# Causal rounds with two key projections one step further apart, and a norm's constant added by GpSimd

## The chip, the cores and the metric

The kernel runs on one core of a Trainium2 chip. The core has four engines that compute, each with its own instruction queue: TensorE (PE, with PEld for its weight loads), VectorE (DVE), ScalarE (ACT) and GpSimd (POOL). SyncE (SP) issues most DMAs. They meet at semaphores only. The metric is the device time of one execution in microseconds (us), as the median of several runs.

## The reference, cut to what matters

A transformer block over x of shape 4 x 1024 x 128 (four batches, 1024 tokens, 128 features), in this order:

```
mod = (silu(c) @ wmod)                       # six 128-vectors per batch: sa, ca, ga, sb, cb, gb
h = layernorm(x) * (1 + ca) + sa             # "norm 1"
x = x + ga * attention_1(h)                  # one head of width 128, no mask, all 1024 keys
h = layernorm(x) * (1 + cb) + sb             # "norm 2", first part (eps 1e-5)
y = rmsnorm(h) * g1                          # "norm 2", second part (eps 1e-6)
h = h + attention_2(y) @ wo                  # causal, 16 query heads, 4 key heads of width 64, rotary
h = h + moe(rmsnorm(h) * g2)                 # 8 experts, one of two picked per token
x = x + gb * h
```

layernorm is (x - mean) / sqrt(var + eps) over the 128 features, and rmsnorm is x / sqrt(mean(x*x) + eps). The rotary part multiplies q by a cosine table and a half-swapped q by a sine table, and adds the two; the same for k.

## The kernel before

The kernel goes through four stages: a start (modulation, norm 1 of batch 0), attention 1 over 32 query tiles (to about 237 us), 16 causal rounds (238 to 1108 us), and the routing with the experts (to the end). The change touches the rounds and the norms.

**Rounds.** One round is one batch and one key head with its four query heads. It has 36 steps, nine for a query head. In each step PE computes four 128x128 blocks of scores (`scoresB`, L1199 to L1203), ACT takes the exponential (L917) and copies it to 16 bit (L905), POOL subtracts the copy to get the low half (L707), and five steps later PE multiplies both halves with the values (`values_parts`, L1221 to L1223, two halves of a step each).

**Side work.** Beside this a round prepares the next one, and finishes the one before, in *entries* that are spread over its steps by tables: "max" (scores again, for the row maxima; PE L1125 and L1128, DVE L1608 or L1610), "k", "q", "r", "v" (projections for the next round: keys, queries, the rotated part, values; PE L1113 or L1107), "turn" and "out" (output projection of the round before), "row" (the maxima transposed; read by ACT, L897). The table `PROJ` gives the step of each projection:

```
PROJ = {0: ("k", 0), 1: ("k", 1), 3: ("q", 0, 0), 5: ("r", 0, 0), 7: ("q", 0, 1), 9: ("r", 0, 1), 11: ("v",),
HIGH_AT = {4: 0, 12: 1, 22: 2}
LOW_AT = {5: 0, 15: 1, 25: 2}
```

PE fills a PSUM bank for each entry and DVE reads it in the same order. There are three side banks. Entry number i of a round uses bank i modulo 3, and PE may fill it only when entry i - 3 has been read. So the order of entries sets who waits for whom:

| | steps 0 to 9, entries in order (E: maxima of the head after next, pieces 0 to 5; L: of the next head, pieces 6 to 9) |
|---|---|
| before | L6 k0, L7 k1, L8, L9 q00, E0, E1 r00 row, E2, E3 q01, E4 E5, L6 r01 |
| after | L6 k0, L7, L8 k1, L9, E0 q00, E1 row, E2 r00, E3, E4 E5 q01, L6 r01 |

Commas part the steps; k0 and k1 are the two halves of the keys. Reading a k entry takes three DVE instructions (L1583, L1585, L1587), q one (L1597), r two (L1600, L1602), a max one. In a step with one entry PE does the scores, both halves of the values, then the entry. With two or more it does the scores, the first entry, the first half of the values, the second entry, the second half, and what is left.

`HIGH_AT` and `LOW_AT` say at which step ACT (`high_half`, L876) and POOL (`low_half`, L680) split the finished keys (number 0) and queries (1, 2) into high and low halves; then SP copies them into place by DMA (`spread_k`, `spread_q`). Between these SP sends each head's row of maxima (`spread_row`, L481), which the next head's first scores wait for.

**Norms.** Each norm is a chain over engines: DVE centres (L1373, L1376), ACT squares (L759, L776), DVE sums the squares of each token, scales the sum by 1/128 and adds eps (`variance`, L1383 and L1386), POOL raises it to the power -0.5 (`power`, L595), DVE multiplies (L1406, L1426). There are twelve such chains: norm 1 of four batches, and both parts of norm 2 of four batches. Seven run in the start and in attention 1, five in the rounds. `NORM_V`, `NORM_A` and `NORM_P` say at which round and step DVE, ACT and POOL take their part: DVE's `variance` stands at step 4 of rounds 0 and 1, step 24 of round 3, step 28 of round 6 and step 14 of round 8; other DVE parts at step 4 of rounds 2, 6 and 7.

Of the kernel before, what the change touches and what calls it, by code (L numbers as in the profile page):

```python
# [12 lines left out]
ALU = mybir.AluOpType  # L13
ACT = mybir.ActivationFunctionType
AX = mybir.AxisListType

P = 128
B, S, D = 4, 1024, 128
# [15 lines left out]
WE = 2 * HID + 2 * D  # L34
DW = D + 1
LN_EPS, RMS_EPS = 1e-5, 1e-6
A_SCALE = float(1.0 / np.sqrt(8.0).astype(np.float32))
NKV = B * HKV
HALVES = 2
# [32 lines left out]
def reader(entry):  # L72
# [1 line left out]
    return READER[entry[0]]  # L74


PROJ = {0: ("k", 0), 1: ("k", 1), 3: ("q", 0, 0), 5: ("r", 0, 0), 7: ("q", 0, 1), 9: ("r", 0, 1), 11: ("v",),
        13: ("q", 1, 0), 15: ("r", 1, 0), 17: ("q", 1, 1), 19: ("r", 1, 1)}
OUTP = {21: ("turn", 0), 23: ("turn", 1), 25: ("turn", 2), 27: ("turn", 3), 30: ("out", 0), 33: ("out", 1)}

HIGH_AT = {4: 0, 12: 1, 22: 2}
LOW_AT = {5: 0, 15: 1, 25: 2}


INPUT_AT = {0: {29: (1, 0)}, 1: {31: (1, 1)}, 4: {29: (2, 0)}, 5: {31: (2, 1)}, 8: {33: (3, 0)}, 9: {29: (3, 1)}}
# [92 lines left out]
def build(nc, x, cT, wmod, w_qkvT, w_projT, b_proj, g1, g2, w_kv, w_o, router_w, router_b, w_exp, consts,  # L178
          cos_t, sin_t, out):
    ctx = ExitStack()  # L180
    with ctx:
# [3 lines left out]
        def sem(name):  # L185
            return ctx.enter_context(nc.semaphore(name))
# [65 lines left out]
        n1 = tiles(carve(S))  # L252
# [14 lines left out]
        sq1 = tiles(arena[:, 14 * S:15 * S])  # L267
# [5 lines left out]
        sqh = tiles(arena[:, 16 * S:17 * S])  # L273
        sq2 = [tiles(arena[:, 24 * S:25 * S]), tiles(arena[:, 12 * S:13 * S])]
# [46 lines left out]
        st1, st2 = sb("st1", [P, 4, NT]), [sb("st2a", [P, 4, NT]), sb("st2b", [P, 4, NT])]  # L321
        rstd1, rstd2 = sb("rstd1", [P, NT]), [sb("rstd2a", [P, NT]), sb("rstd2b", [P, NT])]
# [5 lines left out]
        epsb = sb("epsb", [P, 2, NT])  # L328
# [34 lines left out]
        n1_V, n1_P, n1_A = sem("norm1_vec"), sem("norm1_pool"), sem("norm1_act")  # L363
        n2_v, n2_n, n2_P, n2_s = [sem("norm2_vec0"), sem("norm2_vec1")], sem("norm2_n"), sem("norm2_gated"), sem("norm2_scaled")
        xsum, n2_pow = sem("x1_with_rows"), [sem("norm2_power0"), sem("norm2_power1")]
        n2_sq, n2_out = [sem("norm2_squares0"), sem("norm2_squares1")], sem("norm2_done")
# [35 lines left out]
        fin, out_done, zero_in, fill_ready = sem("fin"), sem("out_done"), sem("zero_in"), sem("fill_ready")  # L402

        N1V = 4
        own_sum, eps_set = sem("sum_of_squares"), sem("eps_set")
        NCONST, NLATE = 2, 7
        block = ctx.enter_context(nc.Block())

# [179 lines left out]
        def _(pool):  # L588
# [2 lines left out]
            pool.memset(ones16[:, :], 1.0)  # L591
            pool.memset(every[:, :], 1.0).then_inc(e_z, 1)

            def power(dst, st):
                return pool.tensor_tensor(dst[:, :], st[:, 3, :], mhalf, ALU.pow)  # L595

            def norm1_power(c):

                pool.wait_ge(n1_V, N1V * c + 3)
                power(rstd1, st1).then_inc(n1_P, 1)  # L600

            def gated(c):

# [12 lines left out]
            def norm2_power(c, part):  # L616

                pool.wait_ge(n2_v[part], (3 * c + 3, c + 1)[part])
                power(rstd2[part], st2[part]).then_inc(n2_pow[part], 1)

            def scaled(c):

# [96 lines left out]
            for k in range(2):  # L719
# [4 lines left out]
                src = hres[:, 2 * k + 1, :, :]  # L724
# [13 lines left out]
            for t in range(ETILES):  # L738
                k = t % YSLOTS
# [12 lines left out]
        def _(act):  # L752
# [3 lines left out]
            def norm1_squares(c):  # L756

                act.wait_ge(n1_V, N1V * c + 2)
                act.activation(sq1, n1, ACT.Square).then_inc(n1_A, 1)  # L759

            def norm2_squares(c, part):

                if part == 0:
                    act.wait_ge(n2_v[0], 3 * c + 2)
                    if c == 3:
                        act.wait_ge(n2_v[1], 3)
                    src = n2 if c < 2 else hres[:, c, :, :]
                else:
                    act.wait_ge(n2_s, 2 * c + 2)
                    if c > 0:  # L770
                        act.wait_ge(n2_v[1], c)
                    if c >= 2:
                        act.wait_ge(n2_v[0], 3 * c + 3)
                    src = hres[:, c, :, :]
                dst = sqh if (c, part) in ((2, 0), (2, 1), (3, 0), (3, 1)) else sq2[part]
                act.activation(dst, src, ACT.Square).then_inc(n2_sq[part], 1)  # L776

            def norm2_out(c):

# [52 lines left out]
            for t in range(NL):  # L832
                b, i = divmod(t, NT)
                r = t % 3
# [3 lines left out]
                if t >= 3:  # L838
                    act.wait_ge(a_pl, t - 2)
                act.activation(pf0[:, r, :], psS[:, t % 2, :], ACT.Exp, scale=A_SCALE).then_inc(a_E, 1)  # L840
                if 3 <= i < 7 and b + 1 < B:
# [514 lines left out]
        def _(v):  # L1356
# [21 lines left out]
                if cut.stop == NT:  # L1378
                    ins.then_inc(n, 1)

            def variance(n, sq, st, eps):

                v.tensor_reduce(st[:, 2, :], sq, AX.X, ALU.add).then_inc(own_sum, 1)  # L1383
                own_sums[0] += 1
                v.wait_ge(own_sum, own_sums[0])
                v.scalar_tensor_tensor(st[:, 3, :], st[:, 2, :], 1.0 / D, epsb[:, eps, :], ALU.mult, ALU.add).then_inc(n, 1)  # L1386

            own_sums = [0]

            def norm1_a(c):  # L1390

# [6 lines left out]
            def norm1_b(c):  # L1398

                v.wait_ge(n1_A, c + 1)  # L1400
                variance(n1_V, sq1, st1, 0)

            def norm1_c(c):

# [12 lines left out]
            def norm2_b(c):  # L1417

                v.wait_ge(n2_sq[0], c + 1)
                variance(n2_v[0], sq2[0] if c < 2 else sqh, st2[0], 0)  # L1420

            def norm2_c(c, cut=slice(0, NT)):

# [6 lines left out]
            def norm2_d(c):  # L1430

                v.wait_ge(n2_sq[1], c + 1)
                variance(n2_v[1], sq2[1] if c < 2 else sqh, st2[1], 1)

            def part_low(c, k):

# [86 lines left out]
            for t in range(NL):  # L1523
# [18 lines left out]
                if t in (5, 6):  # L1542
                    k = (2, 5)[t - 5]
# [171 lines left out]
            for b in range(B):  # L1715
                src = hres[:, b, :, :]
# [92 lines left out]
            for b in range(B):  # L1809
                r = hres[:, b, :, :]  # L1810
# [22 lines left out]
            for t in range(ETILES):  # L1833
                k = t % 4
# [92 lines left out]
```

## Time and profile before

| | |
|---|---|
| median of 3 runs | 1326.16 us (1324.26 to 1326.85) |
| profiled execution | 1324.32 us, its span 1322.5 us |
| busy share of the span | PE 84%, DVE 80%, POOL 76%, ACT 66% |
| busy us | PE 1116.2, DVE 1053.8, POOL 998.5, ACT 872.8 |

The span goes from the first to the last instruction. A busy share is a mean over four stages that have different limits, so it does not say what a change in one stage is worth. A row of the trace gives the start of an instruction, its duration, its engine, line and operands; in square brackets stands how long the engine was idle before it and whose work ended the idle time.

### The profile page before, as it was taken

Reading aid. Unit: us, or ns where it says so; the run is one execution under the profiler, and the core shown is the slowest. Engines: PE = TensorE matmul, PEld = TensorE weight load, DVE = VectorE, ACT = ScalarE, POOL = GpSimd, SP = SyncE. Lnnn points to the kernel's source line nnn. Section 1 sums busy time; section 2 is a strip of 40 time slices with the busy share of each in tenths; the row PEclk is TensorE's granted clock in tenths of the full one; section 3 lists DMA queues with packets and bytes.
Section 4 is the critical chain, followed back from the end, with each engine's and each line's share of the span. In section 5 each row is a group of like instructions: output and inputs, shape, how many; then the busy total and the mean of one; then the engine's idle time right before and its main releaser. Section 6 shows DMA issues by size and latency. Waiting matters only on the chain.

```text
span 1322.5 us, 36076 instructions
## 1 busy us (share of the span) xinstructions
PE 1116.2 (84%) x14984; PEld 839.5 (63%) x14984; DVE 1053.8 (80%) x2180; ACT 872.8 (66%) x1508; POOL 998.5 (76%) x783
## 2 busy tenths in 40 slices
PE   4979895899999899999999999999999997600891
PEld 2768682566776667767677776776767776600881
DVE  6588765889888898989989889898898875592675
ACT  3656671698888688878888888887888894100330
POOL 3555874698898788989899898798888996226454
PEclk8889998899999899999999999999999999555996
DMA  6240013121222211213112131121211200022793
GB/s 219 50 140 2 2 44 86 42 77 43 71 55 56 61 38 52 58 60 77 38 52 54 49 87 43 53 61 42 77 38 26 62 3 2 0 88 74 219 303 145
DMA packets 49247, 90.85 MB, mean 69 GB/s; under 512 B 8896, under 2 KB 19136, under 8 KB 48832
## 3 DMA queue, kind: packets, MB, share of 16 engines
q1 hardware_dynamic: 46128, 81.21, 21.5%
q0 software_dynamic: 2960, 7.38, 2.1%
q8 instruction: 117, 1.92, 0.6%
q14 instruction: 42, 0.34, 0.1%
HBM read 43.96 MB, written 13.01 MB: 43 GB/s over the span
## 4 chain that ended last, share of the span: by engine, by line
PE 61%; DVE 20%; POOL 7%; issue 4%; SPq 3%; ACT 2%; DMA 2%; POOLq 0%; DVEq 0%; ACTq 0%
PE psT L1125 6%; PE psS L1200 5%; PE psS L1199 5%; PE psT L1113 5%; PE psS L1221 5%; PE psS L1222 5%; PE psS L1223 4%; PE psT L1148 3%; PE psO L1125 3%; PE psO L1200 3%; PE psO L1199 3%; DVE pmax L1608 2%; POOL rows_in L735 2%; DVE psT L1585 2%; DVE arena L1587 2%
## 5 line engine op out<-in xcount | busy, mean ns | idle before, releaser
L707 POOL TENSOR_TENSOR probs<-arena,probs 128x512 f16<-128x512 f32 x576 | 656.7, 1161 | 109.2 <-ACT probs L905 104.9
L905 ACT ACTIVATE probs<-arena 128x512 f16<-128x512 f32 x576 | 362.0, 628 | 14.1
L1221 PE MATMUL psS<-vb,probs 128*128 128x65 f16 x2304 | 302.9, 193 | 3.5 <-POOL probs L707 1.2
L1222 PE MATMUL psS<-vb,probs 128*128 128x64 f16 x2304 | 304.1, 194 | 0.0
L1223 PE MATMUL psS<-vb,probs 128*128 128x65 f16 x2304 | 302.2, 192 | 0.0
L917 ACT ACTIVATE arena<-psS 128x512 f32<-128x512 f32 x384 | 226.1, 589 | 105.9 <-PE psS L1203 59.1
L1221 PEld LDWEIGHTS psS<-vb,probs 128*128 128x128 f16 x2304 | 220.4, 97 | 71.6 <-issue 11.2
L1222 PEld LDWEIGHTS psS<-vb,probs 128*128 128x128 f16 x2304 | 215.7, 97 | 47.7 <-issue 0.5
L1608 DVE TENSOR_REDUCE pmax<-psT 128x1 f32<-128x512 f32 (+1 forms) x311 | 198.1, 641 | 28.9 <-PE psT L1128 14.1
L1223 PEld LDWEIGHTS psS<-vb,probs 128*128 128x128 f16 x2304 | 217.0, 99 | 0.0
L1125 PE MATMUL psT<-arena 128*128 128x512 f16 (+3 forms) x507 | 153.4, 323 | 8.6 <-DVE pmax L1608 4.9
L1200 PE MATMUL psS<-arena 65*128 65x512 f16 (+1 forms) x448 | 158.2, 353 | 0.0
L1199 PE MATMUL psS<-arena 128*128 128x512 f16 (+1 forms) x448 | 156.9, 350 | 0.0
L1608 DVE TENSOR_REDUCE pmax<-psO 128x1 f32<-128x512 f32 (+1 forms) x201 | 134.2, 667 | 23.9 <-PE psO L1125 16.2
L917 ACT ACTIVATE arena<-psO 128x512 f32<-128x512 f32 x192 | 112.5, 586 | 25.2 <-PE psO L1200 16.4
L1113 PE MATMUL psT<-arena,wkv 128*128 128x512 f16 x381 | 105.1, 386 | 20.8 <-DVE arena L1587 19.5
L647 POOL TENSOR_TENSOR probs<-arena,probs 128x1024 f16<-128x1024 f32 x32 | 69.4, 2172 | 55.8 <-ACT probs L847 55.7
L1199 PE MATMUL psO<-arena 128*128 128x384 f16 (+2 forms) x320 | 93.7, 293 | 0.0
L958 ACT ACTIVATE arena<-arena 128x256 f32<-128x256 f32 x40 | 16.7, 418 | 112.8 <-DVE arena L1841 112.7
L1125 PE MATMUL psO<-arena 128*128 128x512 f16 (+2 forms) x261 | 85.7, 341 | 5.4 <-DMA arena<-arena 4.6
L1200 PE MATMUL psO<-arena 65*128 65x384 f16 (+2 forms) x320 | 88.4, 295 | 0.0
L1128 PE MATMUL psT<-maskh,identh 128*128 128x128 bf16 x391 | 79.2, 220 | 0.0
(278 smaller groups left out, 2873.2 us busy)
## 6 DMA issues: line engine op xcount, KB each, us to landing
arena<-arena SPq DMA_DIRECT2D x240, 128.0 KB, 2.4
arena<-w_exp_dram SPq DMA_DIRECT2D x40, 384.0 KB, 4.1
arena<-xnT_d SPq DMA_DIRECT2D x16, 512.0 KB, 3.6
wkv<-w_d SPq DMA_DIRECT2D x16, 352.0 KB, 4.1
rows_in<-arena POOLq DMA_DIRECT2D x1, 2580.0 KB, 20.5
arena<-rows_in SPq DMA_DIRECT2D x40, 64.5 KB, 3.3
arena<-x_dram SPq DMA_DIRECT2D x4, 512.0 KB, 5.2
hres<-x_dram SPq DMA_DIRECT2D x4, 512.0 KB, 5.3
```

The costliest lines, as they stand in the source:

```text
L707: pool.tensor_tensor(pl[:, r, :], pf[:, r, :], ph[:, r, :], ALU.subtract).then_inc(lo_P, 1)
L905: act.activation(ph[:, s % RING, :], pf[:, s % RING, :], ACT.Copy).then_inc(b_hi, 1)
L917: act.activation(pf[:, s % RING, :], score_banks[s % SCORES], ACT.Exp).then_inc(b_exp, 1)
L1113: mm = pe.matmul(dst, wkv[:, p, c, w0:w0 + P], xs[:, p, a, h * 512:(h + 1) * 512], start=(k == 0), stop=(k == 2))
L1125: mm = pe.matmul(dst[:, k * w:(k + 1) * w], qA[:, p, g, i * P:(i + 1) * P], kC[:, p, h * 512:h * 512 + w], start=True, stop=not diag)
L1128: mm = pe.matmul(dst[:, (k + 1) * w - P:(k + 1) * w], identh[:, :], maskh[:, :], start=False, stop=True)
L1199: pe.matmul(dst, kA[:, p, j * P:(j + 1) * P], qA[:, p, g, i0 * P:(i0 + n) * P], start=True, stop=False)
L1200: mm = pe.matmul(dst, kB[0:HD + 1, p, j * P:(j + 1) * P], qB[0:HD + 1, p, g, i0 * P:(i0 + n) * P], start=False, stop=not diag)
L1221: pe.matmul(dst, high, vb[:, p, j, 0:OW], start=first, stop=False, skip_group_check=True)
L1222: pe.matmul(dst[:, 0:HD], high, vb[:, p, j, HD + 2:VW], start=False, stop=False, skip_group_check=True)
L1223: mm = pe.matmul(dst, low, vb[:, p, j, 0:OW], start=False, stop=last, skip_group_check=True)
L1608: ins = v.tensor_reduce(pmax[:, e[1] % 2, at[0]:at[0] + 1], src[:, 0:w], AX.X, ALU.max)
```

## The change

It makes two edits that have nothing to do with each other.

The first moves side work. The second half of the keys (k1) goes from step 1 to 2, the first query entry from 3 to 4, its rotated part from 5 to 6, the third from 7 to 8; the split of the keys into halves goes one step later on ACT and POOL. This holds in rounds 0 to 14; round 15 has no projections.

The second moves work in the norms. ACT squares x times 1/sqrt(128), so the sum of the squares is the mean already. DVE keeps only the sum. The addition of eps, 128x8 elements, goes to POOL, which waits for its own addition before it takes the power. DVE's wait for its own sum goes.

```diff
+ROOT = float(1.0 / np.sqrt(float(D)))
...
-PROJ = {0: ("k", 0), 1: ("k", 1), 3: ("q", 0, 0), 5: ("r", 0, 0), 7: ("q", 0, 1), 9: ("r", 0, 1), 11: ("v",),
+PROJ = {0: ("k", 0), 2: ("k", 1), 4: ("q", 0, 0), 6: ("r", 0, 0), 8: ("q", 0, 1), 9: ("r", 0, 1), 11: ("v",),
...
-HIGH_AT = {4: 0, 12: 1, 22: 2}
-LOW_AT = {5: 0, 15: 1, 25: 2}
+HIGH_AT = {5: 0, 12: 1, 22: 2}
+LOW_AT = {6: 0, 15: 1, 25: 2}
...
-            def power(dst, st):
+            powers = [0]
+
+            def power(dst, st, eps):
+                pool.tensor_tensor(st[:, 3, :], st[:, 2, :], epsb[:, eps, :], ALU.add).then_inc(eps_in, 1)
+                powers[0] += 1
+                pool.wait_ge(eps_in, powers[0])
                 return pool.tensor_tensor(dst[:, :], st[:, 3, :], mhalf, ALU.pow)
...
-                act.activation(sq1, n1, ACT.Square).then_inc(n1_A, 1)
+                act.activation(sq1, n1, ACT.Square, scale=ROOT).then_inc(n1_A, 1)
...
-                act.activation(dst, src, ACT.Square).then_inc(n2_sq[part], 1)
+                act.activation(dst, src, ACT.Square, scale=ROOT).then_inc(n2_sq[part], 1)
...
-            def variance(n, sq, st, eps):
-
-                v.tensor_reduce(st[:, 2, :], sq, AX.X, ALU.add).then_inc(own_sum, 1)
-                own_sums[0] += 1
-                v.wait_ge(own_sum, own_sums[0])
-                v.scalar_tensor_tensor(st[:, 3, :], st[:, 2, :], 1.0 / D, epsb[:, eps, :], ALU.mult, ALU.add).then_inc(n, 1)
+            def variance(n, sq, st):
+
+                v.tensor_reduce(st[:, 2, :], sq, AX.X, ALU.add).then_inc(n, 1)
```

## Rows read from the trace of the kernel before

**Rows 1.** The page's chain that ended last: shares of the span by engine.

```profile
PE 61%; DVE 20%; POOL 7%; issue 4%; SPq 3%; ACT 2%; DMA 2%; POOLq 0%; DVEq 0%; ACTq 0%
```

**Rows 2.** Windows: length, busy us (instructions) by engine, granted clock, DMA share, GB/s.

```profile
445.30:449.30 4.00, 3.98 (x30) 2.93 (x31) 3.42 (x6) 1.23 (x2) 0.61 (x1) 0.50 0.20 45
...
852.60:907.20 54.60, 53.10 (x762) 38.30 (x762) 47.80 (x92) 45.03 (x79) 47.20 (x40) 1.00 0.21 55
```

**Rows 3.** Waits in 250 to 1190 us: who waited, total us, times, longest.

```profile
PE psT L1113 <- DVE arena L1587: 15.5, 14, 1.1
...
PE psT L1125 <- DVE pmax L1608: 4.7, 1, 4.7
```

**Rows 4.** Timeline of PE: the fill of q00 in rounds 3, 4, 11 and 12.

```profile
406.65 0.39 PE L1113 MATMUL psT<-arena,wkv 128*128 128x512 f16 x1 [1.11 <-DVE arena L1587]
...
468.49 0.39 PE L1113 MATMUL psT<-arena,wkv 128*128 128x512 f16 x1 [1.11 <-DVE arena L1587]
...
852.67 0.39 PE L1113 MATMUL psT<-arena,wkv 128*128 128x512 f16 x1 [1.10 <-DVE arena L1587]
...
907.29 0.39 PE L1113 MATMUL psT<-arena,wkv 128*128 128x512 f16 x1 [1.11 <-DVE arena L1587]
```

**Rows 5.** Timeline of PE and DVE in round 11, steps 1 to 4.

```profile
848.71 0.81 PE L1113 MATMUL psT<-arena,wkv 128*128 128x512 f16 x3
...
849.28 0.68 DVE L1587 TENSOR_TENSOR arena<-psT,arena 64x512 f32<-64x512 f32 x1
849.35 0.19 PE L1221 MATMUL psS<-vb,probs 128*128 128x65 f16 x1
...
849.54 0.38 PE L1199 MATMUL psO<-arena 128*128 128x512 f16 x1
...
849.89 0.67 DVE L1608 TENSOR_REDUCE pmax<-psO 128x1 f32<-128x512 f32 x1
...
850.49 0.67 DVE L1583 TENSOR_TENSOR arena<-psT,trig 64x512 f32<-64x512 f32 x1
...
851.93 0.68 DVE L1587 TENSOR_TENSOR arena<-psT,arena 64x512 f32<-64x512 f32 x1
...
852.54 0.41 DVE L1610 TENSOR_REDUCE pmax<-psT 128x2 f32<-128x256 f32 x1
...
854.37 0.38 PE L1125 MATMUL psT<-arena 128*128 128x512 f16 x1
```

**Rows 6.** Timelines of POOL, DVE and PE in round 3, around its step 24.

```profile
431.48 10.10 POOL L707 TENSOR_TENSOR probs<-arena,probs 128x512 f16<-128x512 f32 x9
...
443.61 1.15 POOL L707 TENSOR_TENSOR probs<-arena,probs 128x512 f16<-128x512 f32 x1
...
439.17 1.21 DVE L1383 TENSOR_REDUCE st2b<-arena 128x8 f32<-128x1024 f32 x1
440.42 4.37 DVE L1386 SCALAR_TENSOR_TENSOR st2b<-st2b,epsb 128x8 f32<-128x8 f32 x1
...
445.31 0.39 PE L1125 MATMUL psT<-arena 128*128 128x256 f16 x1 [4.69 <-DVE pmax L1608]
```

**Rows 7.** Source line L1386: durations ns min/median/max, first and last start.

```profile
L1386 DVE SCALAR_TENSOR_TENSOR st2a<-st2a,epsb x4: 167/444/885, 132.5 to 618.0; 128x8 f32<-128x8 f32 x4
L1386 DVE SCALAR_TENSOR_TENSOR st2b<-st2b,epsb x4: 167/168/4374, 171.2 to 707.0; 128x8 f32<-128x8 f32 x4
```

**Rows 8.** Timeline of the start, 0 to 24 us.

```profile
8.85 0.91 POOL L638 TENSOR_TENSOR arena<-arena 128x384 f16<-128x384 f32 x1 [7.27 <-ACT arena L818]
...
13.22 0.17 DVE L1386 SCALAR_TENSOR_TENSOR st<-st,epsb 128x8 f32<-128x8 f32 x1
...
13.54 1.67 POOL L595 TENSOR_TENSOR rstd<-st,cst 128x8 f32<-128x8 f32 x1 [2.41 <-DVE st L1386]
```

**Rows 9.** Groups by line in 250 to 1190 us: DVE instructions with two SBUF inputs.

```profile
L1426 DVE TENSOR_TENSOR hres<-hres,rstd2a 128x512 f32<-128x512 f32 x4 | 2.8, 702 | 0.0
...
L1376 DVE SCALAR_TENSOR_TENSOR hres<-st2a,x 128x512 f32<-128x512 f32 x2 | 2.1, 1068 | 0.0
```

More of the change, by code:

```diff
@@ L404, in build @@
         N1V = 4
-        own_sum, eps_set = sem("sum_of_squares"), sem("eps_set")
+        eps_in, eps_set = sem("eps_added"), sem("eps_set")
         NCONST, NLATE = 2, 7
@@ L599, in norm1_power @@
                 pool.wait_ge(n1_V, N1V * c + 3)
-                power(rstd1, st1).then_inc(n1_P, 1)
+                power(rstd1, st1, 0).then_inc(n1_P, 1)
             def gated(c):
@@ L618, in norm2_power @@
                 pool.wait_ge(n2_v[part], (3 * c + 3, c + 1)[part])
-                power(rstd2[part], st2[part]).then_inc(n2_pow[part], 1)
+                power(rstd2[part], st2[part], part).then_inc(n2_pow[part], 1)
             def scaled(c):
@@ L1379, in centred @@
                     ins.then_inc(n, 1)
-            def variance(n, sq, st, eps):
-                v.tensor_reduce(st[:, 2, :], sq, AX.X, ALU.add).then_inc(own_sum, 1)
-                own_sums[0] += 1
-                v.wait_ge(own_sum, own_sums[0])
-                v.scalar_tensor_tensor(st[:, 3, :], st[:, 2, :], 1.0 / D, epsb[:, eps, :], ALU.mult, ALU.add).then_inc(n, 1)
-            own_sums = [0]
+            def variance(n, sq, st):
+                v.tensor_reduce(st[:, 2, :], sq, AX.X, ALU.add).then_inc(n, 1)
             def norm1_a(c):
@@ L1400, in norm1_b @@
                 v.wait_ge(n1_A, c + 1)
-                variance(n1_V, sq1, st1, 0)
+                variance(n1_V, sq1, st1)
             def norm1_c(c):
@@ L1419, in norm2_b @@
                 v.wait_ge(n2_sq[0], c + 1)
-                variance(n2_v[0], sq2[0] if c < 2 else sqh, st2[0], 0)
+                variance(n2_v[0], sq2[0] if c < 2 else sqh, st2[0])
             def norm2_c(c, cut=slice(0, NT)):
@@ L1432, in norm2_d @@
                 v.wait_ge(n2_sq[1], c + 1)
-                variance(n2_v[1], sq2[1] if c < 2 else sqh, st2[1], 1)
+                variance(n2_v[1], sq2[1] if c < 2 else sqh, st2[1])
             def part_low(c, k):
```

## The prediction

> **What bounds the kernel now.** I read the chain that ended last first: TensorE has 61% of it and VectorE 20%, every other engine under 8% [rows 1]. So a step counts where PE waits. Then windows over the causal rounds: in round 11 PE is busy 53.10 of 54.60 us at the full clock, DVE 47.80, POOL 47.20 and ACT 45.03 [rows 2]. PE is the bound there and DVE is 7 us behind it, so at most 1.5 us a round can come from PE's waits, unless a round has a special one. The view of waits names two [rows 3]. The fill on L1113 waits for L1587, the last of the three DVE instructions that read a key entry: 14 times recorded, 1.11 us each. The timeline says where: it is q00, in every round, and the rounds follow each other by 54.62 us (907.29 - 852.67) [rows 4]. The other is a single wait of 4.7 us, on a max entry in round 3, and from round 3 to round 4 q00 advances by 61.84 us (468.49 - 406.65), 7.2 more than a common round [rows 3, 4]. The edits meet these two places.
>
> **The first edit: the moved entries.** The reader should see in the timeline of round 11 that DVE goes from k0 to L7 to k1 without a pause: k0's read ends at 849.96, L7 runs 849.89 to 850.56, k1 850.49 to 852.61, then L8 [rows 5]. q00 is entry 6 and needs the bank of k1, entry 3; it starts at 852.67, 0.06 after the read ended, and PE has idled 1.10 [rows 4, 5].
>
> After the edit the order is L6 k0 L7 L8 k1 L9 E0 q00. k1 becomes entry 4, which needs the bank of k0. A projection holds PE for 0.64 (848.71 to 849.35), half a step's values for 0.19 (849.35 to 849.54) [rows 5]. Step 1 loses the projection, so step 2's scores start at 849.54 - 0.64 = 848.90. Before k1's fill then stand the scores, one max entry and one half of the values, under a step's 1.5 us (54.62 / 36): PE arrives at about 849.7 and waits until k0 is read, to 849.96 + 0.06 = 850.02: a new stall of 0.3. The fill is complete 0.81 later, at 850.83. DVE has by then done L7 and (0.41) L8, to 850.90, and reads k1 for 2.12 (850.49 to 852.61 before), to 853.0. q00 is filled from 853.06, later than before, but with E0 and all of step 4's scores behind it. Compared at the end of step 4: before, E0 starts at 854.37 and is one 512-column matmul, a third of 0.64, so 854.58. After, 853.06 + 0.64 + 0.19 = 853.89. That is 0.69 gained of a wait of 1.1: the chain of DVE reads k0, L7, L8, k1 now sets the pace, and the rest goes into two stalls of about 0.3.
>
> What is late next: row (entry 9) needs E0's read and r00 (entry 11) needs E1's read, which now stand behind q00's read on DVE, a few hundredths too late; I take off 0.05 in all and keep 0.65. From step 9 on the entries are the same as before.
>
> Not all rounds get it. At step 4 of rounds 2, 6 and 7 DVE does norm work of 0.70 to 1.21 us (a half of L1426, or a reduction like L1383) [rows 6, 9]. It stands ahead of E1's read. Before, r00 needed q00's bank, read earlier; now it needs E1's, and PE, which has 0.1 to spare there, waits the 0.6 to 1.1 out. I count 0 for these three rounds (bounds -0.5 and +0.65). Rounds 0 and 1 have a norm's sum there, but lose L1386 behind it (0.17 to 0.885) [rows 7]: 0.5 each. So 10 x 0.65 + 2 x 0.5 = 7.5. The bounds: 0, if every later stall gives it back, and 15 x 1.11 = 16.6, if the wait goes without another.
>
> The moved split of the keys I cost at nothing. ACT and POOL have 9.6 and 7.4 us to spare in the round [rows 2], and the low halves are used five steps later. On SP the three key DMAs stay behind the first row and ahead of the second; they are wanted at step 22, 16 steps on. On ACT the split now stands ahead of the row's read in step 5; this row is wanted in step 9, over 4 us later (4 x 1.5 less the split). If that cover is gone, each us of delay there is paid 15 times.
>
> **The second edit: the norm's constant.** DVE loses twelve L1386. Usually one is 0.17, but one takes 4374 ns [rows 7]: in round 3 it starts at 440.42 and ends at 444.79, and POOL's unbroken run of instructions from 431.48 ends at 444.76 [rows 6]. It reads two small tensors from SBUF. For this time DVE reads no entry, and PE idles 4.69. It also costs clock: in the 4 us after, the granted clock is 0.50, the 1.2 GHz level [rows 2, 6].
>
> Here a rule of the Trainium skill can be set beside the row. The page "SBUF — State Buffer", section "Who interferes with whom", says that a VectorE instruction with two SBUF inputs and a GpSimd instruction that reads SBUF need the same read interface, and that the one issued second is blocked until the first is through. The wait's end at POOL's idle moment agrees in kind; its length doesn't, since several POOL instructions end within it. By the rule alone the wait could be no longer than one POOL instruction, 1.15 here, the second edit would be worth some 1 us, and the time would be 1318; the rule also speaks against the change, since POOL's new addition reads SBUF and can be blocked in its turn. The sum goes by the 4.37.
>
> The sum over the squares (1.21) stays in step 24 of round 3. DVE has little room there, so I leave 1.0 of the 7.2 for it (bounds 0 and 1.21) and count 6.2. Two shorter waits (0.885 in one st2a row, and one between it and the median 0.444) add 0.3: 6.5 in all. A row of reductions shows no such wait, so what DVE keeps isn't exposed.
>
> POOL gains twelve additions of 128x8, of which the trace has none. From above, the power of the same size: 1.67 [rows 8]. From below 0. A subtraction takes 0.91 for 384 elements a partition and 1.15 for 512 [rows 6, 8], 1.9 ns an element over a constant of 0.19; I take 0.2, and 0.1 for the wait behind it. It is on the path once, in the start: the sum ends about 13.2, the power starts at 13.54 after L1386 [rows 8], and would start at about 13.6: +0.1 (bound +1.5). What is queued behind the wait on POOL is the power and then a subtraction of the round, wanted five steps on; 7.4 us of room cover it. The seven L1386 taken off DVE ahead of the rounds (0.17 each) I count at nothing; at best 1.2.
>
> **Sum.** -7.5 - 6.5 + 0.1 = -13.9. The profiled execution took 1324.32 (span 1322.5), 1.84 below the median; it would take 1310.4. Against the median of 1326.16: 1312.3, so 1312.
>
> **Rivals.**
> (a) The wait for k1 goes without another. For it: PE's idle 1.1 is the only one of note in a round. Against: DVE's chain, which is unbroken. 16.6 + 6.5: 1303.
> (b) What q00 gains is given back at r00 and after, because DVE has the same work in these steps and no gap. For it: rounds 2, 6 and 7 as worked out. Against: PE's idle is 1.5 of a round, DVE's 6.8 [rows 2]. Then the second edit alone: 1326.2 - 6.4 = 1320.
> (c) The long wait isn't gone but falls on another instruction. Six DVE instructions with two SBUF inputs stay in rounds 2, 6 and 7, at means of 702 and 1068 ns [rows 9], and every one meets POOL at another moment now. Against: the six show no long wait. One at the old price: 1312 + 7 = 1319.
> (d) Slower: the same mechanism, several times or longer. One wait costs 7.2 by round 3; the second uses up the gain, from the third on the kernel is slower: 1312 + 21.6 = 1334. For it: nothing in the code keeps these six off POOL's runs. Against: one long wait among all those seen.
> That the 4.37 us was an accident of one execution speaks little: the runs lie within 2.6 us, less than such a wait costs.
>
> **Chances.** The forecast 0.57 (1307 to 1317 by its own bounds), (a) 0.10, (b) 0.15, (c) 0.13, (d) 0.05. Two tenths of a per cent, 2.7 us, is about what a measurement tells from no change. The forecast and (a) are faster; of (b) and (c) a quarter could come within it. Faster 0.88, same 0.07, slower 0.05. The range from 1303 to 1322 holds the forecast, half of (a) and most of (b) and (c).
>
> **What would show it.** In the timeline of a round: k1's fill at step 2 right after k0's read, and PE idle of about 0.3 before k1 and before q00 instead of 1.1; q00 to q00 54.0 instead of 54.62 in rounds 11 to 14, and about as before in rounds 2, 6 and 7. Round 3 near 55, with no DVE instruction over 2 us and no granted clock of 0.50 in it. POOL's additions near 0.2. The prediction is wrong if round 3 still has an idle of some us, if common rounds keep their 54.62, or if a DVE instruction of rounds 2, 6 or 7 takes several us.

## The result, and the profile after

The changed kernel took 1310.49 us (median of 4 runs, 1309.2 to 1311.32), the kernel before 1326.47 beside it: a ratio of 0.9879, with a 95% interval from 0.9865 to 0.9894. The forecast was 1312. The profiled execution of after took 1311.32, its span is 1309.5; before it was 1324.32 and 1322.5, so the two traces differ by 13.0. The medians differ by 16.0: the profiled execution of before was the fastest of its four, that of after the slowest.

First the page's chain that ended last, and the window of one common round (round 11) of after. Columns as in [rows 1, 2].

```profile
PE 61%; DVE 20%; POOL 7%; issue 4%; SPq 3%; ACT 3%; DMA 2%; POOLq 0%; DVEq 0%; ACTq 0%
...
836.98:890.98 54.00, 53.32 (x763) 38.34 (x762) 47.83 (x90) 44.90 (x80) 47.25 (x40) 1.00 0.21 55
```

TensorE still sets the end, with the same share. In the common round it idles 0.7 instead of 1.5; its busy time is 0.2 longer, so the idle time shrank by more than the round did. The two waits of [rows 3] are gone from the view of waits, 250 to 1190 us. The longest waits of matmuls that are left on these lines (L1119 and L1131, which were L1113 and L1125) are these:

```profile
PE psO L1119 <- DVE pmax L1609: 3.0, 5, 0.9
...
PE psT L1131 <- DVE pmax L1611: 2.1, 8, 0.3
```

The timeline of PE in rounds 3, 4, 11 and 12 shows the fill of q00, against [rows 4]:

```profile
408.21 0.82 PE L1119 MATMUL psT<-arena,wkv 128*128 128x512 f16 x3
...
463.21 0.82 PE L1119 MATMUL psT<-arena,wkv 128*128 128x512 f16 x3
...
843.37 0.82 PE L1119 MATMUL psT<-arena,wkv 128*128 128x512 f16 x3
...
897.33 0.82 PE L1119 MATMUL psT<-arena,wkv 128*128 128x512 f16 x3
```

None has an idle time beside it; the view shows those over 0.15 us only. From round 11 to 12 it advances by 53.96 (54.62 before), from round 3 to 4 by 55.00 (61.84 before). Around step 24 of round 3 the timelines of DVE and POOL, and a window of 12 us that holds the step in both kernels, show why (the first window is of before, the second of after; compare [rows 6]):

```profile
434.00:446.00 12.00, 7.31 (x101) 5.59 (x98) 11.86 (x17) 7.11 (x13) 10.77 (x9) 0.89 0.28 65
```

```profile
434.00:446.00 12.00, 11.49 (x166) 8.52 (x165) 11.83 (x23) 10.13 (x19) 12.00 (x11) 1.00 0.24 57
...
439.66 1.21 DVE L1389 TENSOR_REDUCE st2b<-arena 128x8 f32<-128x1024 f32 x1
440.79 0.55 DVE L1609 TENSOR_REDUCE pmax<-psT 128x1 f32<-128x384 f32 x1
...
430.89 11.24 POOL L713 TENSOR_TENSOR probs<-arena,probs 128x512 f16<-128x512 f32 x10
```

The sum (L1389) again falls into an unbroken run of POOL, but the maximum behind it starts at once. PE is busy 11.49 of the 12 us instead of 7.31, and the clock stays at the 2.4 GHz level.

By stages, from the first exponential of one round to that of the next, the time went here (this table and the next are worked out from the starts of the exponentials in each trace; us):

| | before | after | difference |
|---|---|---|---|
| ahead of the rounds | 238.36 | 241.49 | +3.1 |
| rounds 4, 5, 9 to 14, each | 54.22 to 55.09 | 53.54 to 54.42 | -0.65 to -0.68 |
| round 3 | 61.83 | 55.00 | -6.83 |
| rounds 0, 1, 8 | 51.80, 55.81, 56.00 | 51.01, 54.77, 55.13 | -0.79, -1.04, -0.87 |
| rounds 2, 6, 7 | 54.36, 55.10, 54.76 | 54.22, 54.75, 54.63 | -0.14, -0.35, -0.13 |
| all rounds | 868.20 | 852.72 | -15.5 |
| behind the rounds | 215.94 | 215.28 | -0.7 |

Round 0 differs between executions of one kernel: a second trace of after (e11) has 51.51 for it, and 853.24 for all rounds. So the rounds gave 15.0 to 15.5, and some 3 was lost ahead of them, where the prediction had 0.1. The experiments had to say which edit gave what, whether the long wait was an accident, what takes part in it, and what the 3.1 is.

### The profile page after: what moved, and what is told of

Same layout as the page of the kernel before. It is cut to its first block, busy times and chain, and to the rows that moved or that the text cites. A ratio compares the mean times of both kernels' runs of the same rounds, so it can differ in the third digit from the quotient of the medians.

```text
span 1309.5 us, 36076 instructions
## 1 busy us (share of the span) xinstructions
PE 1118.2 (85%) x14984; PEld 839.0 (64%) x14984; DVE 1048.1 (80%) x2168; ACT 870.7 (66%) x1508; POOL 1000.8 (76%) x795
## 4 chain that ended last, share of the span: by engine, by line
PE 61%; DVE 20%; POOL 7%; issue 4%; SPq 3%; ACT 3%; DMA 2%; POOLq 0%; DVEq 0%; ACTq 0%
PE psT L1131 6%; PE psS L1206 5%; PE psS L1205 5%; PE psS L1227 5%; PE psS L1228 4%; PE psT L1119 4%; PE psS L1229 4%; PE psT L1154 3%; PE psO L1206 3%; PE psO L1205 3%; PE psO L1131 3%; DVE pmax L1609 3%; POOL rows_in L741 2%; PE psO L1119 2%; DVE psT L1586 2%
## 5 line engine op out<-in xcount | busy, mean ns | idle before, releaser
L1609 DVE TENSOR_REDUCE pmax<-psT 128x1 f32<-128x512 f32 (+1 forms) x341 | 218.8, 645 | 26.3 <-PE psT L1134 13.6
L1131 PE MATMUL psT<-arena 128*128 128x512 f16 (+3 forms) x507 | 158.1, 330 | 2.7 <-DVE pmax L1611 2.1
L1609 DVE TENSOR_REDUCE pmax<-psO 128x1 f32<-128x512 f32 (+1 forms) x171 | 113.6, 664 | 19.0 <-PE psO L1131 12.8
L1119 PE MATMUL psT<-arena,wkv 128*128 128x512 f16 x336 | 92.8, 387 | 7.7 <-DVE arena L1588 2.7
L1131 PE MATMUL psO<-arena 128*128 128x512 f16 (+3 forms) x261 | 80.6, 327 | 5.2 <-DMA arena<-arena 4.8
L1134 PE MATMUL psT<-maskh,identh 128*128 128x128 bf16 x361 | 73.4, 220 | 0.0
```

The lines of the kernel that those rows point to most:

```text
L1119: mm = pe.matmul(dst, wkv[:, p, c, w0:w0 + P], xs[:, p, a, h * 512:(h + 1) * 512], start=(k == 0), stop=(k == 2))
L1131: mm = pe.matmul(dst[:, k * w:(k + 1) * w], qA[:, p, g, i * P:(i + 1) * P], kC[:, p, h * 512:h * 512 + w], start=True, stop=not diag)
L1134: mm = pe.matmul(dst[:, (k + 1) * w - P:(k + 1) * w], identh[:, :], maskh[:, :], start=False, stop=True)
L1609: ins = v.tensor_reduce(pmax[:, e[1] % 2, at[0]:at[0] + 1], src[:, 0:w], AX.X, ALU.max)
```

## Experiments

All are compared with before on the same chip. Lengths of some rounds for all of them (us):

| | ahead | round 1 | 3 | 6 | 7 | 11 | all rounds |
|---|---|---|---|---|---|---|---|
| before | 238.36 | 55.81 | 61.83 | 55.10 | 54.76 | 54.62 | 868.20 |
| after | 241.49 | 54.77 | 55.00 | 54.75 | 54.63 | 53.97 | 852.72 |
| e1 moves alone | 238.22 | 54.97 | 60.33 | 54.75 | 54.62 | 53.96 | 858.52 |
| e2 norms alone | 242.67 | 54.90 | 55.67 | 55.10 | 54.78 | 54.63 | 860.77 |
| e3 moves, scalar eps | 239.27 | 54.97 | 60.36 | 54.75 | 54.63 | 53.97 | 859.80 |
| e4 keys later | 240.10 | 54.09 | 55.17 | 54.06 | 54.27 | 54.12 | 851.81 |
| e5 probe, two inputs | 240.15 | 70.88 | 71.61 | 71.86 | 70.10 | 68.20 | 1077.23 |
| e6 probe, one input | 239.85 | 55.38 | 55.52 | 55.54 | 55.31 | 54.40 | 860.41 |
| e7 sum earlier | 241.95 | 55.81 | 61.43 | 55.10 | 54.78 | 54.63 | 867.52 |
| e8 norms elsewhere | 237.50 | 55.17 | 54.05 | 54.64 | 58.01 | 53.96 | 855.55 |
| e9 both orders | 240.06 | 54.10 | 54.05 | 54.07 | 54.27 | 53.97 | 848.92 |
| e10 addition twice | 241.91 | 54.77 | 55.00 | 54.76 | 54.63 | 53.97 | 852.68 |
| e11 after again | 241.09 | 54.77 | 55.00 | 54.76 | 54.62 | 53.97 | 853.24 |

**e1, the moves alone**: before with the tables of after.

```diff
-PROJ = {0: ("k", 0), 1: ("k", 1), 3: ("q", 0, 0), 5: ("r", 0, 0), 7: ("q", 0, 1), 9: ("r", 0, 1), 11: ("v",),
+PROJ = {0: ("k", 0), 2: ("k", 1), 4: ("q", 0, 0), 6: ("r", 0, 0), 8: ("q", 0, 1), 9: ("r", 0, 1), 11: ("v",),
...
-HIGH_AT = {4: 0, 12: 1, 22: 2}
-LOW_AT = {5: 0, 15: 1, 25: 2}
+HIGH_AT = {5: 0, 12: 1, 22: 2}
+LOW_AT = {6: 0, 15: 1, 25: 2}
```

> The moved entries alone, norms as before. Theory of the forecast (two independent edits): common rounds 53.96 us instead of 54.62, rounds 2, 6, 7 as before, so about -8 us: 1318.5. Round 3 keeps its long L1386: the rounds before it are shorter, but the order of the instructions within round 3 from step 9 on and its distances to POOL's run are the same, so the wait is 4.4 us again and round 3 is near 61. Rival (the wait is an accident of the moment, and any shift removes it): round 3 near 55 and -15 us, 1312. Rival (the moves alone explain nothing): 1326.

Measured: 1315.26 us, ratio 0.9927 (0.9906 to 0.9949); rounds -9.7. The six runs fall into two groups, 1312.5 to 1312.9 and 1317.6 to 1320.2, so the lengths from the trace say more than this median. The common rounds have the 53.96 of after, and round 3 keeps the wait although everything ahead of it has moved. The timeline of DVE in round 3:

```profile
437.93 4.40 DVE L1386 SCALAR_TENSOR_TENSOR st2b<-st2b,epsb 128x8 f32<-128x8 f32 x1
```

The profiled run is of the lower group (1312.82), so the wait isn't what parts the groups; what does is open.

**e2, the norms alone**: after with the tables of before (the diff of e1, turned round).

> The norm's edit alone, entries as before. Theory: common rounds 54.62 as before, PE idle 1.1 before q00 in each; round 3 near 55.6 with no DVE instruction over 2 us; attention 1 longer by 0.3 at each of three POOL powers (0.85 in all); about -6: 1320.5. Rival (the second edit does more than round 3, e.g. less DVE work in all the stages): under 1317. Rival (the clock in 205 to 240 us is lower because of this edit, so 3 us are lost ahead of the rounds): first causal round 3 us later than before, and 1323.

Measured: 1317.15 us, ratio 0.993 (0.9916 to 0.9944); rounds -7.4, of which 6.16 in round 3, and common rounds as before. The two edits alone make 17.1 in the rounds, together 15.5. The difference lies in rounds 3 and 1, where each gains a part of the same idle time (round 1: -0.84 and -0.91 alone, -1.04 together; round 3: -1.50 and -6.16, together -6.83).

**e7, the sum earlier**: before, with round 3's sum of squares in another step.

```diff
-NORM_V = {..., 3: {24: ("d", 2)},
+NORM_V = {..., 3: {19: ("d", 2)},
```

> The kernel before, with one number changed: the sum of round 3 stands at step 19 instead of 24, amid another unbroken run of POOL. Theory (the 4.4 us belong to the moment at which L1386 came, not to its being there): it takes 0.17 to 1.2, round 3 is near 55.5 instead of 61.8, -6 us: 1319.5 to 1320, what the second edit gave in the rounds. Rival (any L1386 inside POOL's run waits for its end): 3 to 6 us at step 19 too, no gain: 1325.

Measured: 1324.79 us, ratio 0.9975 (0.9958 to 0.9992). Five steps earlier, the timelines of DVE and POOL have it again:

```profile
436.91 4.57 DVE L1386 SCALAR_TENSOR_TENSOR st2b<-st2b,epsb 128x8 f32<-128x8 f32 x1
...
433.62 7.83 POOL L707 TENSOR_TENSOR probs<-arena,probs 128x512 f16<-128x512 f32 x7
```

The wait ends at 441.48, 0.03 after POOL's run (433.62 + 7.83). So the one other step that was tried, amid another run of POOL, doesn't avoid it. Three of the twelve runs took 1316 to 1318; whether they lacked the wait can't be told, since there is no trace of them.

Why POOL's run ends there can be read from before, in the timelines of POOL and ACT behind [rows 6]:

```profile
448.69 1.16 POOL L707 TENSOR_TENSOR probs<-arena,probs 128x512 f16<-128x512 f32 x1 [3.93 <-ACT probs L905]
...
447.36 0.60 ACT L917 ACTIVATE arena<-psS 128x512 f32<-128x512 f32 x1 [5.83 <-PE psS L1200]
```

POOL had no work left: it waited for ACT, ACT for PE's scores, and PE for the DVE that POOL's run had held up. In e1, e3 and e7 POOL's next instruction comes 3.9 to 5.7 us later as well, released by ACT. So in these four the wait lasted until the stall that it caused had emptied POOL's queue. No semaphore is part of it: DVE's wait lies inside its instruction, although the engines were said to meet at semaphores only.

**e3, one SBUF input**: e1, with the eps as an immediate, so that the instruction reads one small tensor.

```diff
-v.scalar_tensor_tensor(st[:, 3, :], st[:, 2, :], 1.0 / D, epsb[:, eps, :], ALU.mult, ALU.add).then_inc(n, 1)
+v.tensor_scalar(st[:, 3, :], st[:, 2, :], 1.0 / D, (LN_EPS, RMS_EPS)[eps], ALU.mult, ALU.add).then_inc(n, 1)
```

> The moved entries, and eps added on DVE as before but by an instruction with one SBUF input (two constants in place of the small eps tensor); POOL has no addition. Theory (the long wait belongs to DVE instructions with two SBUF inputs): L1386 takes 0.17 in all twelve places, round 3 is near 55, and attention 1 isn't longer by 0.3 three times: 1 us below the changed kernel, 1309.5. Rival (any small DVE instruction between two SBUF tensors meets POOL's run): 4 us in round 3 again, 1318.

Measured: 1315.93 us, ratio 0.9929 (0.9912 to 0.9946): no better than e1. The source line, and the timelines of DVE, POOL and PE in round 3:

```profile
L1386 DVE TENSOR_SCALAR st2b<-st2b x4: 170/172/4454, 170.3 to 703.5; 128x8 f32<-128x8 f32 x4
...
440.21 4.45 DVE L1386 TENSOR_SCALAR st2b<-st2b 128x8 f32<-128x8 f32 x1
...
443.45 1.19 POOL L707 TENSOR_TENSOR probs<-arena,probs 128x512 f16<-128x512 f32 x1
...
445.18 0.39 PE L1125 MATMUL psT<-arena 128*128 128x256 f16 x1 [4.76 <-DVE pmax L1608]
```

The wait is as long as with two inputs, and again it ends when POOL does (444.64). The page "SBUF — State Buffer" of the Trainium skill, section "Who interferes with whom", says more than the prediction took from it: tensor_scalar too can enter a mode that takes the ports shared with GpSimd, where its operands meet certain conditions, while tensor_reduce never does. Both halves agree with the runs (4.45 here; e6 below for the reduction).

**e5 and e6, a probe of the wait**: after, with one more small DVE instruction behind each of the 576 steps; nobody uses what it writes. e5 reads two SBUF tensors, e6 is a reduction of one.

```diff
+if probes[0]:
+    v.wait_ge(probed, probes[0])
+probes[0] += 1
+v.scalar_tensor_tensor(st1[:, 3, :], st1[:, 2, :], 1.0 / D, epsb[:, 0, :], ALU.mult, ALU.add).then_inc(probed, 1)
```

```diff
+v.tensor_reduce(st1[:, 3, :], mhalf.unsqueeze(2), AX.X, ALU.add).then_inc(probed, 1)
```

> The changed kernel, and after each of the 576 steps DVE does one more small instruction of the removed kind (128x8, two SBUF inputs, result unused): 576 samples of its wait against POOL. Theory 1 (it waits for the POOL instruction in flight and no longer): all durations between 0.17 and 1.3 (2.3 beside the 2.13 us splits), a mean of some 0.6. Theory 2 (one that comes in the last 0.1 us of a POOL instruction whose successor has started is passed over until POOL's run ends): most as in theory 1, and some per cent of them from 2 to over 5 us. The kernel is far slower in both, by 100 us or more.

> The same 576 probes with a reduction of one SBUF input, the kind that the changed kernel keeps on DVE. Theory (this kind needs nothing that POOL holds): all 0.15 to 0.2, whatever POOL does; the kernel is 576 x 0.1 to 0.17 of DVE work slower at most, below 1400. Rival (every DVE instruction meets POOL's run): the spread of the other probe.

Measured, one execution each: 1534.32 and 1319.39 us. The source line of the probe in e5, then in e6 (ns min/median/max):

```profile
L1703 DVE SCALAR_TENSOR_TENSOR st<-st,epsb x576: 148/620/6205, 243.2 to 1316.2; 128x8 f32<-128x8 f32 x192
```

```profile
L1703 DVE TENSOR_REDUCE st<-cst x576: 141/151/163, 243.0 to 1099.0; 128x8 f32<-128x8 f32 x192
```

No reduction waited, though 504 of the 576 began while POOL was busy. Of the two-input probes 387 began at least 0.02 us before the end of a POOL instruction and ended after it. 372 of them were through within 0.12 of this end, though in 211 of these the next POOL instruction was already started. The other 15 were passed over at one to three further ends and took 1.8 to 6.2 us. One of them, in the timelines of DVE and POOL in e5:

```profile
455.98 5.96 DVE L1703 SCALAR_TENSOR_TENSOR st<-st,epsb 128x8 f32<-128x8 f32 x1
...
455.27 2.12 POOL L686 TENSOR_TENSOR arena<-arena 64x1024 f16<-64x1024 f32 x1
457.36 2.25 POOL L713 TENSOR_TENSOR probs<-arena,probs 128x512 f16<-128x512 f32 x2
459.58 2.33 POOL L636 TENSOR_TENSOR hres<-hres,mod 128x1024 f32<-128x1024 f32 x1
```

So most waits end with the POOL instruction that is met; a few outlast several. Eleven of the 15 ended with POOL still in its run, so "until POOL is idle" isn't the rule either. They aren't scattered: there is one in each of rounds 0 to 14, at step 6 or 7. Fourteen began beside the split of the keys (L686, 64 partitions, 2.13 us), which only one other probe met; the 30 that met a split of the queries (L688, 128 partitions) were all let in at its end. So 15 of 387 is no rate of chance, but what makes one be passed over stays open.

The condition of theory 2 didn't hold. The waits of before, e1, e3 and e7 began 0.05 to 0.12 before the end of a POOL instruction, and its successor started before that end. Five probes began in this way, 0.05 to 0.07 before the end, and took 0.16 at most; the 15 began 0.69 to 1.67 before it. So e5 shows that a two-input instruction can outlast several POOL instructions, and it doesn't reproduce how the kernel's own long wait began.

**e4, keys still later**: after with k1, q00 and r00 one step later.

```diff
-PROJ = {0: ("k", 0), 2: ("k", 1), 4: ("q", 0, 0), 6: ("r", 0, 0), 8: ("q", 0, 1), 9: ("r", 0, 1), 11: ("v",),
+PROJ = {0: ("k", 0), 3: ("k", 1), 5: ("q", 0, 0), 7: ("r", 0, 0), 8: ("q", 0, 1), 9: ("r", 0, 1), 11: ("v",),
```

> The changed kernel with k1 one step further on (step 3), q00 at 5 and r00 at 7. Theory (what is left in a common round is two waits of 0.13 to 0.3 each for the chain k0, L7, L8, k1 on DVE): k1 finds its bank free and q00 comes later than k1's read, both waits go, common rounds 53.6 to 53.7 instead of 53.96, 10 x 0.3 = 3 us less: 1307.5. Rival (DVE's work in steps 0 to 9 sets the pace, whatever the order): the waits move to q01 and r01, rounds stay at 53.96 or get longer: 1310 to 1316.

Measured: 1311.88 us, ratio 0.9889 (0.987 to 0.9907). Both small stalls are gone, and the common round is 0.15 longer. A new wait stands in step 5; timelines of PE and DVE in round 11:

```profile
841.57 0.19 PE L1227 MATMUL psS<-vb,probs 128*128 128x65 f16 x1 [0.56 <-DVE arena L1648]
...
841.02 0.41 DVE L1648 TENSOR_TENSOR arena<-psS,oinv 128x256 f32<-128x256 f32 x1
```

DVE now reads the last k1 entry ahead of the output of a finished head (L1648), and the next values need this bank. Rounds 0, 1, 2, 6 and 7 gain (0.44, 0.68, 0.37, 0.69, 0.36): there DVE does norm work in step 4, and q00 and r00 now miss it. (For round 0 the 0.44 is no more than two executions of after differ by.)

**e8, the norms elsewhere**: after, with the constant added by DVE ahead of the rounds, the norms of rounds 1, 2, 6 and 7 in other steps, and round 3's sum at step 30 (its power at 33; POOL's table is left out below).

```diff
+                v.tensor_reduce(st[:, 2, :], sq, AX.X, ALU.add).then_inc(own_sum, 1)
+                own_sums[0] += 1
+                v.wait_ge(own_sum, own_sums[0])
+                v.tensor_tensor(st[:, 3, :], st[:, 2, :], epsb[:, eps, :], ALU.add).then_inc(n, 1)
...
-NORM_V = {0: {4: ("d", 1)}, 1: {4: ("b", 2)}, 2: {4: ("c", 2, 0), 13: ("c", 2, 1)}, 3: {24: ("d", 2)},
-          6: {4: ("a", 3), 11: ("a_centre", 3, 0), 17: ("a_centre", 3, 1), 28: ("b", 3)},
-          7: {4: ("c", 3, 0), 13: ("c", 3, 1)}, 8: {14: ("d", 3)}}
+NORM_V = {0: {4: ("d", 1), 31: ("b", 2)}, 1: {31: ("c", 2, 0)}, 2: {13: ("c", 2, 1)}, 3: {30: ("d", 2)},
+          5: {33: ("a", 3)}, 6: {11: ("a_centre", 3, 0), 17: ("a_centre", 3, 1), 28: ("b", 3)},
+          7: {10: ("c", 3, 0), 13: ("c", 3, 1)}, 8: {14: ("d", 3)}}
```

> The changed kernel with two corrections. In the start and attention 1, where no long wait was seen, eps is added on DVE again, without POOL's addition; and the norm work at step 4 of rounds 1, 2, 6 and 7 goes to steps 31, 31, 33 (of the rounds before) and 10, the sum of round 3 to step 30. Theory: attention 1 shorter by 0.85; rounds 1, 2, 6, 7 lose their extra waits of 0.87, 0.35, 0.87 and 0.35, round 3 its 0.5: -3 in all, 1307.5. Rival (DVE's work only waits elsewhere): -0.85 alone, 1309.6.

Measured: 1311.84 us, ratio 0.9897 (0.9881 to 0.9913), no better than after. Round 3 gained 0.95 and round 2 0.53, round 6 only 0.11, round 1 lost 0.40 and round 7 3.4. Timelines of DVE, POOL and PE there:

```profile
632.63 3.65 DVE L1437 TENSOR_TENSOR hres<-hres,rstd2a 128x512 f32<-128x512 f32 x1
...
630.12 5.61 POOL L715 TENSOR_TENSOR probs<-arena,probs 128x512 f16<-128x512 f32 x5
...
636.67 0.39 PE L1133 MATMUL psT<-arena 128*128 128x512 f16 x1 [1.53 <-DVE pmax L1621]
```

This is L1426 of [rows 9], 0.70 there. It got in when POOL's run ended at 635.73, 0.55 before its own end: as in round 3, on another instruction. It is the prediction's rival (c), with one of these six moved to step 10, among other moves.

**e9, both orders**: after, with e4's order in rounds 0, 1, 2, 6 and 7, round 3's sum at step 30, and the constant added by DVE ahead of the rounds as in e8.

```diff
+BUSY = (0, 1, 2, 6, 7)
...
+    proj = PROJ_BUSY if it in BUSY else PROJ
...
-NORM_V = {..., 3: {24: ("d", 2)},
+NORM_V = {..., 3: {30: ("d", 2)},
```

> Three corrections to the changed kernel. (1) In rounds 0, 1, 2, 6 and 7 the entries stand with k1 at step 3, q00 at 5 and r00 at 7 (the order that was better there, by 0.44, 0.68, 0.37, 0.69 and 0.36 us); the other rounds keep k1 2, q00 4, r00 6. (2) Round 3's sum of squares goes from step 24 to 30 and its power from 30 to 33. (3) Up to the first causal round the constant is added by VectorE behind the sum, not by GpSimd ahead of the power. Theory: the three places are separate, so their gains add up: 2.5 us from (1), 0.9 from (2), 0.8 or more in attention 1 from (3): 4.2 below the changed kernel, about 1306.5, rounds about 849.3 long. Rival: an order of one round changes how the next begins, or a two-input instruction of VectorE meets a GpSimd run at another place again: then one round is 3 us longer and the kernel is no better than the changed one, about 1310.

**e11, after again**, beside it.

> The changed kernel unchanged, beside the corrected one on the same chip. Theory: rounds 852.7 us as in its first profile and 0.988 of the kernel before; what lies ahead of the rounds (241.5 us in the first profile) changes by some 2 us with the granted clock between 200 and 240 us, which the three profiles of kernels with the same work there have shown at 0.50 and at 1.00. Rival: the clock there is the change's own doing: 0.50 from 205 to 215 us again.

Measured: e9 1306.38 us (1301.62 to 1307.63), ratio 0.9844 (0.9822 to 0.9866); after again 1312.26, ratio 0.9895 (0.9876 to 0.9914). So e9 is the fastest, 5.9 us below after at the medians. Its rounds came out at 848.92 where 849.3 was expected, rounds 1, 2, 6 and 7 within 0.01 of e4, round 0 0.35 below it, and round 3 as in e8: these gains do add up. The same window of round 3 in e9 has no idle PE left:

```profile
434.00:446.00 12.00, 12.00 (x185) 9.37 (x181) 10.96 (x22) 10.30 (x19) 12.00 (x11) 1.00 0.29 68
```

**e10, the addition twice**: after, with POOL's addition made twice.

```diff
                 pool.tensor_tensor(st[:, 3, :], st[:, 2, :], epsb[:, eps, :], ALU.add).then_inc(eps_in, 1)
+                pool.wait_ge(eps_in, 2 * powers[0] + 1)
+                pool.tensor_tensor(st[:, 3, :], st[:, 2, :], epsb[:, eps, :], ALU.add).then_inc(eps_in, 1)
```

> The changed kernel with GpSimd's addition of the constant made twice ahead of every power (the second writes the same value again). Theory: in attention 1 each of the later powers stands on the path that TensorE waits for, so the second addition costs again what the first did, 0.25 to 0.3 us at each of three places (about 0.85 in all up to 197 us), and nothing in the rounds. Rival: the 0.85 us that the changed kernel lost in attention 1 has another cause (VectorE's shorter work, a clock), and doubling the addition moves nothing there (under 0.2 us up to 197 us).

Measured: 1309.51 us, one execution. Two powers of attention 1 stand on POOL with one subtraction between; the timelines of POOL in before, after and e10:

```profile
174.63 1.65 POOL L595 TENSOR_TENSOR rstd2b<-st2b,cst 128x8 f32<-128x8 f32 x1
...
178.33 1.64 POOL L595 TENSOR_TENSOR rstd2a<-st2a,cst 128x8 f32<-128x8 f32 x1
```

```profile
175.51 1.65 POOL L601 TENSOR_TENSOR rstd2b<-st2b,cst 128x8 f32<-128x8 f32 x1
...
179.21 0.21 POOL L598 TENSOR_TENSOR st2a<-st2a,epsb 128x8 f32<-128x8 f32 x1
179.49 1.64 POOL L601 TENSOR_TENSOR rstd2a<-st2a,cst 128x8 f32<-128x8 f32 x1
```

```profile
175.64 1.65 POOL L603 TENSOR_TENSOR rstd2b<-st2b,cst 128x8 f32<-128x8 f32 x1
...
179.89 1.64 POOL L603 TENSOR_TENSOR rstd2a<-st2a,cst 128x8 f32<-128x8 f32 x1
```

From one power to the next it is 3.70, 3.98 and 4.25: each addition costs 0.28 there, 0.20 of its own and 0.08 for the wait behind it. On PE it shows as well. Taking the same instructions of PE in two traces, those of after come 0.28 later against before's at 145 us than at 130, and again 0.27 later at 180 than at 170. e2, e5, e6 and e11 have the same two steps, e1, e3, e7, e8 and e9, without POOL's addition there, have none over 0.03. At the second step e10 has 0.56, twice as much, as the theory says. Around the first it can't be compared: its PE was 2.0 ahead of e11's at 130 us and had lost that by 167, for a reason that stays open.

What lies in the 3.1 ahead of the rounds: 0.55 by these two steps, each behind a power. A third, behind the power at 91 us, would make up the 0.87 by which PE is later at 197 us; but there the kernels without the addition move by -0.3 to +0.3 too, so it isn't shown. The rest, 2.3, comes between 197 us and the rounds. A window of 205 to 210 us, behind attention 1, in before, in e7 and in after:

```profile
205.00:210.00 5.00, 2.37 (x36) 2.05 (x36) 1.67 (x6) 0.13 (x1) 1.11 (x1) 1.00 0.00 0
```

```profile
205.00:210.00 5.00, 3.36 (x30) 2.83 (x27) 0.87 (x3) 1.06 (x1) 2.15 (x2) 0.50 0.00 0
```

```profile
205.00:210.00 5.00, 3.17 (x28) 2.64 (x26) 1.04 (x4) 0.98 (x1) 1.97 (x1) 0.50 0.00 0
```

The clock stood at 2.4 GHz in the profiled execution of before and at 1.2 in that of after. All eight traces with 0.50 in this window lose 1.84 against before within it (by the starts of the same PE instructions), e1 and e9 with 1.00 and 0.94 nothing. But e7 does up to round 3 exactly what before does, and its execution had 0.50 there too. It reached the rounds at 241.95, 3.6 later than before's: 1.0 by 197 us and 2.6 from there on. So a loss of this size comes without the change. Whether the change makes it likelier stays open: of the kernels with POOL's addition in attention 1 all five had 0.50 there, and the two probes on top of it 0.57; of the six without it three had 0.50 (e3, e7, e8). e11's theory that the clock would change in after itself found no support: 0.50 again. So its rival, and the similar one of e2, aren't refuted.

## Why the prediction was right

**The first edit** was sized well: 0.65 for a common round, measured 0.65 to 0.68 in eight of ten (round 8 gave 0.87, round 3 is below), and e1 shows that it is this edit alone. The walk through the banks holds too. The timelines of PE and DVE in round 11 of after, to be set beside [rows 5]:

```profile
837.28 0.81 PE L1119 MATMUL psT<-arena,wkv 128*128 128x512 f16 x3
840.32 0.82 PE L1119 MATMUL psT<-arena,wkv 128*128 128x512 f16 x3
...
839.58 0.68 DVE L1588 TENSOR_TENSOR arena<-psT,arena 64x512 f32<-64x512 f32 x1
840.19 0.67 DVE L1609 TENSOR_REDUCE pmax<-psO 128x1 f32<-128x512 f32 x1
840.78 0.41 DVE L1611 TENSOR_REDUCE pmax<-psT 128x2 f32<-128x256 f32 x1
...
842.63 0.68 DVE L1588 TENSOR_TENSOR arena<-psT,arena 64x512 f32<-64x512 f32 x1
```

k0's read ends at 840.26 (839.58 + 0.68) and k1 is filled from 840.32; k1's read ends at 843.31 and q00 is filled from 843.37, 0.06 later each time. From k0's fill to q00's it is 6.09; before it was 5.68, and the walk put q00 0.39 later (853.06 against 852.67), which is 6.07. PE's idle before the two fills is 0.13 and 0.14, half of the 0.3 forecast each (0.69 gained of 1.1 had left 0.4 for both); DVE's unbroken chain sets the pace, as said. The idle before r00 in the rounds with norm work is 0.87 in rounds 1 and 6 and 0.35 in 2 and 7. It is the stall that was counted at 0.6 to 1.1 for 2, 6 and 7, mostly smaller, so that these gain 0.13 to 0.35 instead of 0. Rounds 0 and 1 gave 1.8 instead of 1.0 (1.3 by the trace of e11).

**The second edit**: 6.2 for round 3, measured 6.17 (6.83 less a common 0.66), and 6.16 in e2. Leaving 1.0 to the sum fits as well: moving the sum to step 30 gave 0.95. Of the 0.3 for two shorter waits, the 0.885 was counted twice: it is round 1's L1386 and stood in that round's 0.5 already. That the wait is a stable part of before, and no accident of one execution, is now shown by e1, e3 and e7, whose traces all have it, at 4.40 to 4.57. The reason given for it was only half right: "It reads two small tensors from SBUF" isn't what decides, since e3 waits as long with one.

**The mis-sized term** is POOL's addition, "on the path once, in the start: +0.1". In the start the power comes at 13.60 instead of 13.54, but at 13.53 in e11, so no cost stands out there. Two more stand on the path in attention 1, where I looked for room only in the rounds: 0.55 in all, and a third may. At one of them GpSimd is blocked in its turn, as the Trainium skill's rule had threatened; timelines of POOL and DVE in after, then of POOL in before:

```profile
136.65 1.18 POOL L598 TENSOR_TENSOR st2a<-st2a,epsb 128x8 f32<-128x8 f32 x1
...
135.81 1.96 DVE L1407 TENSOR_TENSOR arena<-arena,rstd 128x1024 f32<-128x1024 f32 x1
```

```profile
136.05 2.62 POOL L595 TENSOR_TENSOR rstd2a<-st2a,cst 128x8 f32<-128x8 f32 x1
```

The addition took 1.18 instead of 0.20 and ended 0.06 after the DVE instruction. But in before the power was held up here by as much, 2.62 instead of 1.65, so this wait is no cost of the change: PE is 0.28 later behind it, as at the other place. The rule of that section, that the one issued second waits for the first, agrees with these rows and with 372 of 387 probes; it doesn't cover the 15 others, nor round 3, where the edit gave 6.2 instead of the 1 or so by that rule.

**The rivals.** (a), that the wait for k1 goes without another, fell: two small waits took its place, and e4, which removes them, meets a third. (b) fell with e1. (c) and (d) didn't happen in after, but e8 shows that they were live: with one of the six instructions six steps later, a long wait was back, at half of (c)'s price (3.4 of 7).

**The number** is in part luck. In the traces the rounds gave 1.5 more than the 14.0 counted and the stage behind them 0.7, while 3.0 more than counted was lost ahead of them: 13.0 in all, with 13.9 forecast. The medians give 16.0, and 14.5 in the second measurement of after (e11).

## What to carry to other kernels

When an instruction takes over twenty times its median, look at what the neighbour engine runs at that moment; here an operation of another kind (a reduction) or another engine removed the wait, where another step and one tensor operand fewer didn't. An order of entries that shares banks is best chosen per round: the gain of each order depended on what else the reading engine did in that step, and e9 took the better of two in each. An addition that moves to another engine costs its length plus its wait in every stage where that engine is on the path, so the stages should be walked one by one.

## What the runs showed of the hardware that was not expected

- A DVE instruction on 128x8 elements can be passed over at several ends of POOL instructions: 15 of 387 probes that met one, up to 6.2 us, the rest let in at the first end. The 15 are one in each round, 14 beside a split of 64 partitions. Why these is open.
- A tensor_scalar with two immediates waited once like an instruction with two SBUF inputs (4.45 us); 576 reductions of 128x8 never did (at most 163 ns).
- On POOL an addition of 128x8 takes 0.20 us, its power of -0.5 1.65.
- The granted clock between 205 and 215 us differs from execution to execution for the same work (1.00 in before, 0.50 in e7), and with it the time from 197 us to the rounds by 2.6 us.
